# Layer 2 attention with probabilities left unnormalised: reciprocal sums spread, transposed and multiplied into the heads

## The chip, the cores and the metric

The kernel runs on one core of a Trainium2 chip. It is one program for four layers of a small transformer. The metric is the device time of one execution in microseconds (us). Its engines work in parallel, each through its own queue in order, and meet at semaphores: PE is TensorE (matrix products and transposes, from SBUF to the eight PSUM banks), DVE is VectorE, ACT is ScalarE, POOL is GpSimd, SP issues transfers.

## The reference

Activations are four batch rows of 512 tokens and 128 channels. Each layer has an attention and a feed-forward part, each behind a layer norm with modulation and a gate. The change touches only the attention of layer 2, with 16 heads of 64:

```python
q = apply_rope(split_heads(x @ Wq)); k = apply_rope(split_heads(x @ Wk)); v = split_heads(x @ Wv)
sim = jnp.einsum('bid,bjd->bij', q, k) * scale
sim = jnp.where(causal[None], sim, -jnp.inf)
attn = jax.nn.softmax(sim, axis=-1)
out = jnp.einsum('bij,bjd->bid', attn, v)
out = out.reshape(b, h, t, d).transpose(0, 2, 1, 3).reshape(b, t, h * d)
return out @ Wo + bo
```

## The kernel before

The stage works in 32 units, one for each batch row (`B` = 4) and pair of heads (`PAIRS` = 8). In a unit, 128 partitions hold two heads of 64 channels, and the 512 tokens are four tiles of 128 (`TB` = 4). The software pipeline is written out by hand: in round u of every engine's loop (from -2 to 32) unit u+2 is projected, unit u+1 gets its scores and exponentials, unit u is transposed and multiplied with the values, and unit u-1 is projected out and added to the residual `x`. The source's order is the order of each queue; the only other order is by the semaphores.

The steps, by their functions:

- `att_project` (L991, L994): q, k (one 512-wide product each) and v (four 128-wide ones) into bank 0. `att_rope` on DVE (L1124, L1125) multiplies and swaps out of bank 0, and POOL (L1201, L1206) multiplies and adds to `q_rope` and `k_rope`.
- `att_scores` (L1007): causal scores of both heads, in three steps of 512 keys (query tile 3), 384 and 128 (tiles 2 and 0) and 256 (tile 1), into banks 1 to 4. `att_maxes` on DVE (L1134) masks and takes row maxima. `att_exps` on ACT (L1079) writes exponentials to `soft` and row sums to `exp_sum`.
- `norm`: on DVE (L1152 reciprocal, L1145 product) for the first head and half of the second; on POOL (L1215) for tiles 3 and 2 of the second. It scales `soft` in place.
- `att_transpose` (L1021): the 20 blocks of 128x128 below the diagonal, in five groups f = 0 to 4 (`FILLS`) of four blocks. Group n of the whole run goes into bank 5 + n % 2; ACT copies it to `softT` (L1091).
- `att_values` (L1033): values of both heads into bank 7, channels by tokens. DVE copies them to `head_out` (L1164, `heads`).
- `att_output` (L1039): output projection of the pair, bank 7 again; DVE adds it to `x` with the gate (L1174, `add`; L1170 adds the bias once per batch row).

So the order of PE in round u is: scores step 0 of u+1, q projection of u+2, output of u-1, transposes f = 0 of u, scores step 1, f = 1, k projection, f = 2, scores step 2, f = 3, v projection, f = 4, values.

Of the kernel before, what the change touches and what calls it, by code (L numbers as in the profile page):

```python
# [20 lines left out]
B = 4  # L21
# [41 lines left out]
def adaln_blocks(nc, d, out):  # L63

    ctx = ExitStack()
    with ctx:
# [899 lines left out]
        exp_sum = tmp_sb("exp_sum", [128, 2, 8])  # L966
        exp_inv = tmp_sb("exp_inv", [128, 2, 8])
        head_out = [tmp_sb(f"head_out{i}", [128, T]) for i in range(2)]
# [43 lines left out]
        def att_transpose(pe, u, f):  # L1012
            if f < 2:
                pe.wait_ge(sem("p_normed"), 2 * u + f + 1)
            if f == 1:
                pe.wait_ge(sem("p_normed_pool"), u + 1)
            if 5 * u + f >= 2:
                pe.wait_ge(sem("pt_ready"), 5 * u + f - 1)
            for i, (hd, jc, t) in enumerate(FILLS[f]):
                at = TILE_AT[t] + 128 * jc  # L1020
                last = pe.transpose(bank[5 + (5 * u + f) % 2][:, 128 * i:128 * i + 128],  # L1021
                                    soft[u % 2][:, hd, at:at + 128], ident[:, :])
            last.then_inc(sem("pt_raw"), 1)

        def att_values(pe, u):
            if u:
                pe.wait_ge(sem("pair_added"), added(u - 1))
            pe.wait_ge(sem("proj_read"), 3 * u + 3)
            for jc, fills in ((0, 2), (1, 4), (3, 4), (2, 5)):
                pe.wait_ge(sem("pt_ready"), 5 * u + fills)  # L1030
# [53 lines left out]
        def att_act(act):  # L1084
            nc.scalar.preload_act_table_set("natural_log_exp_and_others")

            def transposed(u, f):
                if f == 0 and u:
                    act.wait_ge(sem("pv_raw"), B + u)
                act.wait_ge(sem("pt_raw"), 5 * u + f + 1)  # L1090
                nc.scalar.activation(softT[:, 512 * f:512 * f + 512], bank[5 + (5 * u + f) % 2][:, :], ACT.Copy) \  # L1091
                  .then_inc(sem("pt_ready"), 1)

            def values(u):
                act.wait_ge(sem("proj_raw"), 3 * u + 3)
                if u >= 3:
                    act.wait_ge(sem("pv_raw"), B + u - 2)
                nc.scalar.activation(v_tok[u % 3][:, :, :], bank[0][:, :].rearrange("p (i c) -> p i c", i=TB),
                                     ACT.Copy).then_inc(sem("proj_read"), 1)

            for u in range(-2, UNITS + 1):
                score, project, work = 0 <= u + 1 < UNITS, u + 2 < UNITS, 0 <= u < UNITS
                if score:
                    att_exps(act, u + 1, 0)
                if work:
                    transposed(u, 0)
                    transposed(u, 1)
                if score:
                    att_exps(act, u + 1, 1)
                if work:  # L1110
                    transposed(u, 2)
                    transposed(u, 3)
                if score:
# [23 lines left out]
        def att_dve(dve):  # L1137
            def norm(u):
                par = u % 2

                def tiles(hd, ts):
                    for t in ts:
                        n = stat_at(t, hd)
                        p = soft[par][:, hd, TILE_AT[t]:TILE_AT[t] + keys(t)]
                        last = nc.vector.tensor_scalar(p, p, exp_inv[:, par, n:n + 1], None, ALU.mult)  # L1145
                    return last

                if u >= 2:
                    dve.wait_ge(sem("p_normed_pool"), u - 1)
                for half in range(2):  # L1150
                    dve.wait_ge(sem("s_exp"), 8 * u + STEP_END[1 + half])
                    nc.vector.reciprocal(exp_inv[:, par, 4 * half:4 * half + 4], exp_sum[:, par, 4 * half:4 * half + 4]) \  # L1152
                      .then_inc(sem("s_inv"), 1)
                    dve.wait_ge(sem("s_inv"), 2 * u + half + 1)
                    if half == 0:
                        tiles(0, (3, 2))
                tiles(0, (0, 1)).then_inc(sem("p_normed"), 1)
                tiles(1, (0, 1)).then_inc(sem("p_normed"), 1)
# [20 lines left out]
            for u in range(-2, UNITS + 1):  # L1179
                score, project, out = 0 <= u + 1 < UNITS, u + 2 < UNITS, u >= 1  # L1180
                if out:
                    heads(u - 1)
                if score:
# [3 lines left out]
                if out:  # L1187
                    add(u - 1)
                if score:
                    att_maxes(dve, u + 1, 1)  # L1190
                if project:
                    att_rope(dve, u + 2, 1)
                if score:
                    att_maxes(dve, u + 1, 2)
                    norm(u + 1)

        def att_pool(pool):
# [11 lines left out]
            pool.wait_ge(sem("att_tables"), 32)  # L1209
            def norm(u):  # L1210
                pool.wait_ge(sem("s_inv"), 2 * u + 1)
                for t in (3, 2):
                    n = stat_at(t, 1)
                    p = soft[u % 2][:, 1, TILE_AT[t]:TILE_AT[t] + keys(t)]
                    last = nc.gpsimd.tensor_tensor(p, p, exp_inv[:, u % 2, n:n + 1].to_broadcast([128, keys(t)]), ALU.mult)  # L1215
                last.then_inc(sem("p_normed_pool"), 1)

            for u in range(UNITS):
                rope(u, 0)
                rope(u, 1)  # L1220
                if u >= 1:
                    norm(u - 1)
            norm(UNITS - 1)

# [1041 lines left out]
```

## Time and profile before

| | us |
|---|---|
| median of 3 runs | 1713.69 (1708.1 to 1717.39) |
| the profiled execution | 1712.15 |
| its span in the profile | 1710.3 |

| engine | busy us | share of the span | instructions |
|---|---|---|---|
| PE | 1280.4 | 75% | 10366 |
| DVE | 1093.0 | 64% | 2509 |
| ACT | 829.1 | 48% | 2019 |
| POOL | 623.6 | 36% | 577 |

The layer 2 attention is the stretch from about 382 to 782 us of the span. The shares above are averages over stages with different limits, so this stage has to be read by itself. In a timeline a row is a run of like instructions: its start, the time from the first start to the last end, how many, and in brackets what ended an idle time. An fp32 product shows as two instructions on PE, and a next one starts before the one ahead of it has ended, so the distance between starts tells how long a group holds the engine.

### The profile page before, as it was taken

How to read it: one execution, taken by the hardware profiler on the slowest of the kernel's cores; microseconds unless marked ns; L12 is line 12 of the kernel's file. 1: busy time of each engine (PE TensorE's matmuls, PEld its weight loads, DVE VectorE, ACT ScalarE, POOL GpSimd, SP SyncE). 2: the span in 40 equal slices, each digit the busy share in tenths (PEclk: the TensorE clock that was granted, in tenths of full speed). 3: DMA queues.
4: the chain of work that ended last, by engine and by line, in shares of the span. 5: the costliest groups of instructions: out<-in, count | busy, mean ns of one | idle time of the engine just before them, and what ended most of it. 6: DMA issues, size and time to landing. Idle time of an engine off the chain costs nothing.

```text
span 1710.3 us, 27876 instructions
## 1 busy us (share of the span) xinstructions
PE 1280.4 (75%) x10366; PEld 734.0 (43%) x10366; DVE 1093.0 (64%) x2509; ACT 829.1 (48%) x2019; POOL 623.6 (36%) x577
## 2 busy tenths in 40 slices
PE   8754009548999999996878888767777687777768
PEld 6222009514555555552345555434444433444433
DVE  4366503227999999994257777646776644677653
ACT  4651003124566665664666666545555434555542
POOL 1110160345565565652012222145555404555520
PEclk8966559757999999998999999869999997999989
DMA  7000115560000000002000000000000000000000
GB/s 252 1 0 0 48 40 202 125 69 1 1 1 1 1 1 1 1 1 87 0 1 2 2 2 2 1 27 1 2 2 2 2 1 1 2 2 2 1 2 25
DMA packets 15265, 38.95 MB, mean 23 GB/s; under 512 B 3572, under 2 KB 8054, under 8 KB 14496
## 3 DMA queue, kind: packets, MB, share of 16 engines
q1 hardware_dynamic: 13088, 34.70, 5.7%
q0 software_dynamic: 2048, 2.54, 2.1%
q8 instruction: 80, 1.31, 0.3%
q14 instruction: 49, 0.40, 0.1%
HBM read 33.07 MB, written 5.77 MB: 23 GB/s over the span
## 4 chain that ended last, share of the span: by engine, by line
PE 37%; DVE 31%; ACT 15%; issue 10%; POOL 4%; DMA 1%; SPq 0%; DVEq 0%; POOLq 0%; ACTq 0%
DVE soft L1145 6%; DVE bank L1134 5%; PE bank L1694 4%; PE bank L1377 4%; ACT win_soft_alibi L1384 3%; PE bank L1359 3%; ACT win_soft_local L1384 3%; PE bank L1916 3%; DVE rope_part L1125 3%; PE bank L1349 2%; PE bank L195 2%; ACT win_softT_alibi L1392 2%; PE bank L1702 2%; PE bank L1713 2%; PE bank L203 2%
## 5 line engine op out<-in xcount | busy, mean ns | idle before, releaser
L1079 ACT ACTIVATE soft<-bank,neg_max 128x512 f32<-128x512 f32 (+3 forms) x256 | 133.2, 535 | 123.9 <-DVE neg_max L1134 122.7
L1863 POOL TENSOR_TENSOR win_part<-win_part,scaled_tab 128x512 f32<-128x512 f32 x64 | 81.2, 1269 | 200.7 <-DVE win_part L1805 200.7
L1145 DVE TENSOR_SCALAR soft<-soft,exp_inv 128x128 f32<-128x128 f32 (+1 forms) x192 | 137.5, 768 | 2.2
L1694 PE MATMUL bank<-shifted,att_w 128*128 128x512 f32 x128 | 78.9, 748 | 78.2 <-DVE v_even L1832 69.1
L1201 POOL TENSOR_TENSOR rope_part<-rope_part,rope_tab 128x512 f32<-128x512 f32 x64 | 82.2, 1285 | 145.9 <-DVE rope_part L1125 145.8
L1419 POOL TENSOR_TENSOR win_soft_alibi<-win_soft_alibi,win_inv_alibi 128x384 f32<-128x384 f32 x64 | 52.9, 827 | 218.3 <-DVE win_inv_alibi L1403 218.3
L1134 DVE CUSTOM_DVE_ANT_0 bank<-bank,att_mask 128x512 f32<-128x512 f32 (+3 forms) x256 | 118.5, 512 | 6.9 <-PE bank L1007 6.9
L1091 ACT ACTIVATE softT<-bank 128x512 f32<-128x512 f32 x160 | 93.6, 612 | 26.5 <-PE bank L1021 26.5
L1021 PE MATMUL bank<-ident,soft 128*128 128x128 f32 x640 | 99.7, 279 | 1.9 <-ACT softT L1091 1.9
L1007 PE MATMUL bank<-k_rope,q_rope 64*128 64x128 f32 (+3 forms) x512 | 97.6, 479 | 2.2 <-POOL k_rope L1206 2.2
L1384 ACT ACTIVATE win_soft_local<-bank,win_neg_max_local,rq 128x128 f32<-128x128 f32 x256 | 96.2, 463 | 5.7 <-DVE win_neg_max_local L1815 5.7
L1419 POOL TENSOR_TENSOR win_soft_local<-win_soft_local,win_inv_local 128x512 f32<-128x512 f32 x64 | 78.7, 1231 | 55.1 <-DVE win_inv_local L1403 55.1
L1021 PEld LDWEIGHTS bank<-ident,soft 128*128 128x128 f32 x640 | 74.0, 141 | 50.0 <-issue 42.7
L1751 ACT ACTIVATE win_sq_local<-bank 128x512 f32<-128x512 f32 x64 | 38.2, 597 | 112.0 <-PE bank L1694 112.0
L251 DVE TENSOR_TENSOR ln_norm<-bank,ln_rstd 128x512 f32<-128x512 f32 x40 | 27.7, 692 | 100.2 <-ACT ln_rstd L239 94.9
L1392 ACT ACTIVATE win_softT_local<-bank 128x512 f32<-128x512 f32 x64 | 38.3, 598 | 107.1 <-PE bank L1359 107.1
L1392 ACT ACTIVATE win_softT_alibi<-bank 96x512 f32<-96x512 f32 x64 | 38.3, 598 | 87.6 <-PE bank L1359 87.6
L264 POOL TENSOR_SCALAR h<-ln_norm,mod 128x512 f32<-128x512 f32 x28 | 22.0, 785 | 152.6 <-DVE ln_norm L251 152.6
L1033 PE MATMUL bank<-softT,v_tok 128*64 128x128 f32 (+3 forms) x512 | 76.0, 439 | 0.0
L991 PE MATMUL bank<-h,att_w 128*128 128x512 f32 x128 | 72.4, 649 | 4.1 <-DVE ln_norm L251 2.2
L1804 DVE TENSOR_TENSOR win_part<-bank,scaled_tab 128x512 f32<-128x512 f32 x64 | 44.0, 687 | 49.0 <-ACT win_sq_local L1751 49.0
L1691 PE MATMUL bank<-att_w,shifted 128*128 128x128 f32 x256 | 40.0, 303 | 43.2 <-ACT log_q L1758 43.2
(329 smaller groups left out, 3331.0 us busy)
## 6 DMA issues: line engine op xcount, KB each, us to landing
moe_w<-in_moe_w SPq DMA_DIRECT2D x8, 960.0 KB, 6.1
y_tok<-in_moe_w SPq DMA_DIRECT2D x8, 960.0 KB, 5.6
att_w<-in_att_w SPq DMA_DIRECT2D x1, 1536.0 KB, 8.3
att_w<-in_local_w SPq DMA_DIRECT2D x1, 1536.0 KB, 8.9
xg_dram<-zeros SPq DMA_DIRECT2D x5, 256.0 KB, 9.2
y_dram<-y_slot SPq DMA_DIRECT2D x16, 80.0 KB
wmod<-in_wmod SPq DMA_DIRECT2D x1, 1152.0 KB, 7.6
x<-in_x SPq DMA_DIRECT2D x4, 256.0 KB, 4.6
```

The costliest lines, as they stand in the source:

```text
L1007: last = pe.matmul(score_bank(u, s, hd)[:, at:at + keys(t)], q_rope[u % 2][lo:lo + 64, 128 * t:128 * t + 128], k_rope[u % 2][lo:lo + 64, 0 ...
L1021: last = pe.transpose(bank[5 + (5 * u + f) % 2][:, 128 * i:128 * i + 128], soft[u % 2][:, hd, at:at + 128], ident[:, :])
L1079: nc.scalar.activation(soft[par][:, hd, TILE_AT[t]:TILE_AT[t] + keys(t)], score_bank(u, s, hd)[:, at:at + keys(t)], ACT.Exp, scale=-1.0, b ...
L1091: nc.scalar.activation(softT[:, 512 * f:512 * f + 512], bank[5 + (5 * u + f) % 2][:, :], ACT.Copy) \
L1134: nc.vector.tensor_tensor_reduce(sc, sc, att_mask[:, T - keys(t):T], -1.0, 3e38, ALU.add, ALU.min, neg_max[:, u % 2, n:n + 1]).then_inc(se ...
L1145: last = nc.vector.tensor_scalar(p, p, exp_inv[:, par, n:n + 1], None, ALU.mult)
L1201: nc.gpsimd.tensor_tensor(rope_part[2 * piece + 1][:, :], rope_part[2 * piece + 1][:, :], rope_tab[:, 2 * piece + 1, :], ALU.mult).then_in ...
L1384: nc.scalar.activation(a["soft"][u % 2][:, j, :], bank[2 + half][:, 128 * k:128 * k + a["keys"]], ACT.Exp, bias=a["neg_max"][:, u % 2, j:j ...
L1392: nc.scalar.activation(a["softT"][0:a["keys"], 512 * half:512 * half + 512], bank[4 + 3 * half][0:a["keys"], :], ACT.Copy).then_inc(sem("w ...
L1419: nc.gpsimd.tensor_tensor(a["soft"][u % 2][:, js, :], a["soft"][u % 2][:, js, :], a["inv"][:, u % 2, js].unsqueeze(2).to_broadcast([128, 4 ...
L1694: last = pe.matmul(bank[5 * piece][:, :], w, tokens(b, 0, T), start=True, stop=True)
L1863: nc.gpsimd.tensor_tensor(swapped, swapped, scaled_tab[:, 2 * j + 1, :], ALU.mult) \
```

## The change

The exponentials stay unnormalised. DVE takes one reciprocal of the eight row sums of a unit (`invert`). POOL spreads them to `inv_wide`, 64 copies of each, so that four tiles of 128 partitions (queries) by 128 (two heads by 64) stand there (`spread`). PE transposes these four tiles into bank 6 (`att_sums`), ACT copies bank 6 to `sum_inv`, channels by tokens (`inverse`), and DVE multiplies the heads by it where it copied them before (`heads`). Bank 5 now takes f = 0, 2 and 4, bank 6 takes f = 1, 3 and the sums. The copy of f = 3 moves from ACT to DVE (`transposed` there). The output projection moves from ahead of f = 0 to behind f = 1. On DVE, `heads` moves behind the q rope and `add` behind the maxima of step 1.

```diff
         def att_transpose(pe, u, f):
-            if f < 2:
-                pe.wait_ge(sem("p_normed"), 2 * u + f + 1)
-            if f == 1:
-                pe.wait_ge(sem("p_normed_pool"), u + 1)
-            if 5 * u + f >= 2:
-                pe.wait_ge(sem("pt_ready"), 5 * u + f - 1)
+            if f == 0:
+                pe.wait_ge(sem("s_exp"), 8 * u + 8)
+            if f == 1 and u:
+                pe.wait_ge(sem("sum_inv"), u)
+            elif u or f > 1:
+                pe.wait_ge(sem("pt_ready"), 4 * u + max(f - 1, 0))
...
+        def att_sums(pe, u):
+            pe.wait_ge(sem("inv_spread"), u + 1)
+            for t in range(TB):
+                last = pe.transpose(bank[6][:, 128 * t:128 * t + 128], inv_wide[:, stat_at(t, 0):stat_at(t, 0) + 2, :].rearrange("p i c -> p (i c)"), ident[:, :])
+            last.then_inc(sem("sum_raw"), 1)
...
+                if jc == 1:
+                    pe.wait_ge(sem("pt_ready_dve"), u + 1)
...
-                if out:
-                    att_output(pe, u - 1)
                 if work:
                     att_transpose(pe, u, 0)
                 if score:
                     att_scores(pe, u + 1, 1)
                 if work:
                     att_transpose(pe, u, 1)
+                if out:
+                    att_output(pe, u - 1)
...
                     att_values(pe, u)
+                    att_sums(pe, u)
...
+            def inverse(u):
+                act.wait_ge(sem("sum_raw"), u + 1)
+                if u:
+                    act.wait_ge(sem("pv_read"), u)
+                nc.scalar.activation(sum_inv[:, :], bank[6][:, :], ACT.Copy).then_inc(sem("sum_inv"), 1)
...
                 if work:
                     transposed(u, 0)
+                if out:
+                    inverse(u - 1)
+                if work:
                     transposed(u, 1)
...
+            def invert(u):
+                dve.wait_ge(sem("s_exp"), 8 * u + 8)
+                if u:
+                    dve.wait_ge(sem("inv_spread"), u)
+                nc.vector.reciprocal(exp_inv[:, :], exp_sum[:, u % 2, :]).then_inc(sem("s_inv"), 1)
...
             def heads(u):
                 dve.wait_ge(sem("pv_raw"), B + u + 1)
                 if u >= 2:
                     dve.wait_ge(sem("att_out"), u - 1)
-                nc.vector.tensor_copy(head_out[u % 2][:, :], bank[7][:, :]).then_inc(sem("pv_read"), 1)
+                dve.wait_ge(sem("sum_inv"), u + 1)
+                nc.vector.tensor_tensor(head_out[u % 2][:, :], bank[7][:, :], sum_inv[:, :], ALU.mult) \
+                  .then_inc(sem("pv_read"), 1)
...
-                if out:
-                    heads(u - 1)
+                if 0 <= u < UNITS:
+                    invert(u)
                 if score:
                     att_maxes(dve, u + 1, 0)
                 if project:
                     att_rope(dve, u + 2, 0)
                 if out:
-                    add(u - 1)
+                    heads(u - 1)
                 if score:
                     att_maxes(dve, u + 1, 1)
+                if out:
+                    add(u - 1)
                 if project:
                     att_rope(dve, u + 2, 1)
+                if 0 <= u < UNITS:
+                    transposed(u, 3)
                 if score:
                     att_maxes(dve, u + 1, 2)
-                    norm(u + 1)
...
+            def spread(u):
+                pool.wait_ge(sem("s_inv"), u + 1)
+                if u:
+                    pool.wait_ge(sem("sum_raw"), u)
+                nc.gpsimd.tensor_copy(inv_wide[:, :, :], exp_inv[:, :].unsqueeze(2).to_broadcast([128, 8, 64])) \
+                  .then_inc(sem("inv_spread"), 1)
```

Left out above: the normalising on DVE and POOL, which goes; the buffers; the counts of `pt_ready`, now four a unit; and DVE's copy of f = 3, which reads bank 6 and counts `pt_ready_dve`.

On PE, at the start of a round in the middle of the stage, before; L1007 are scores, L991 a q or k projection, L1039 the output projection, L1021 the transposes:

```order
L1007 MATMUL bank<-k_rope,q_rope 128x512 [waits s_exp,roped]
L1007 MATMUL bank<-k_rope,q_rope 128x512
L991 MATMUL bank<-h,att_w 128x512 [waits proj_read]
L1039 MATMUL bank<-head_out,att_wo 128x512 [waits pv_read]
L1021 MATMUL bank<-ident,soft 128x128 [waits pt_ready,p_normed]
L1021 MATMUL bank<-ident,soft 128x128 x3
L1007 MATMUL bank<-k_rope,q_rope 128x384 [waits s_exp]
L1007 MATMUL bank<-k_rope,q_rope 128x384
L1007 MATMUL bank<-k_rope,q_rope 128x128 x2
L1021 MATMUL bank<-ident,soft 128x128 [waits pt_ready,p_normed_pool,p_normed]
```

And after, from the last three of the four transposes of the sums, L1029, at the end of the round ahead; L1009 are the scores, L993 the projections, L1023 the transposes and L1048 the output projection:

```order
L1029 MATMUL bank<-ident,inv_wide 128x128 x3
L1009 MATMUL bank<-k_rope,q_rope 128x512 [waits s_exp,roped]
L1009 MATMUL bank<-k_rope,q_rope 128x512
L993 MATMUL bank<-h,att_w 128x512 [waits proj_read]
L1023 MATMUL bank<-ident,soft 128x128 [waits pt_ready,s_exp]
L1023 MATMUL bank<-ident,soft 128x128 x3
L1009 MATMUL bank<-k_rope,q_rope 128x384 [waits s_exp]
L1009 MATMUL bank<-k_rope,q_rope 128x384
L1009 MATMUL bank<-k_rope,q_rope 128x128 x2
L1023 MATMUL bank<-ident,soft 128x128 [waits sum_inv]
L1023 MATMUL bank<-ident,soft 128x128 x3
L1048 MATMUL bank<-head_out,att_wo 128x512 [waits pv_read]
```

Four transposes stand new at the end of the round, f = 1 waits for the copied sums (`sum_inv`) where it waited for normalised probabilities, and the output projection stands behind it.

On ACT, from the wide exponentials (L1079) of a round, before; L1091 copies transposes:

```order
L1079 ACTIVATE soft,exp_sum<-bank,neg_max 128x512 [waits s_max] x2
L1091 ACTIVATE softT<-bank 128x512 [waits pt_raw,pv_raw]
L1091 ACTIVATE softT<-bank 128x512 [waits pt_raw]
L1079 ACTIVATE soft,exp_sum<-bank,neg_max 128x384 [waits s_max]
L1079 ACTIVATE soft,exp_sum<-bank,neg_max 128x128
```

And after; L1089 are exponentials, L1101 copies transposes and L1115 copies the sums:

```order
L1089 ACTIVATE soft,exp_sum<-bank,neg_max 128x512 [waits s_max] x2
L1101 ACTIVATE softT<-bank 128x512 [waits pt_raw,pv_raw]
L1115 ACTIVATE sum_inv<-bank 128x512 [waits pv_read,sum_raw]
L1101 ACTIVATE softT<-bank 128x512 [waits pt_raw]
L1089 ACTIVATE soft,exp_sum<-bank,neg_max 128x384 [waits s_max]
L1089 ACTIVATE soft,exp_sum<-bank,neg_max 128x128
```

The copy of the sums stands behind the two wide exponentials and the copy of f = 0, and ahead of the copy of f = 1.

## Rows read from the trace of the kernel before

**Rows 1.** Stretches: length, busy PE, PEld, DVE, ACT, POOL (instructions), PEclk, DMA, GB/s.

```profile
900.00:1080.00 180.00, 152.96 (x1945) 90.28 (x1944) 139.49 (x274) 114.32 (x323) 41.36 (x50) 1.00 0.01 2
500.00:594.00 94.00, 92.20 (x524) 50.26 (x522) 93.37 (x256) 58.64 (x176) 55.44 (x49) 1.00 0.00 1
```

**Rows 2.** Chain of waits, 509 to 533, shares by line.

```profile
by line: DVE soft L1145 28.4%; DVE bank L1134 23.4%; issue 12.0%; DVE rope_part L1125 11.9%; DVE rope_part L1124 8.1%; DVE head_out L1164 5.7%; DVE neg_max L1134 4.6%; DVE x L1174 3.3%; DVE x L1170 1.6%; DVE exp_inv L1152 1.2%; DVEq L1173 0
```

**Rows 3.** Timeline of PE, one unit: start, length, instruction, [idle before].

```profile
524.43 1.13 PE L1007 MATMUL bank<-k_rope,q_rope 64*128 64x512 f32 x4
...
526.49 1.12 PE L1039 MATMUL bank<-head_out,att_wo 128*128 128x512 f32 x2
527.45 0.60 PE L1021 MATMUL bank<-ident,soft 128*128 128x128 f32 x4
527.98 1.14 PE L1007 MATMUL bank<-k_rope,q_rope 64*128 64x384 f32 x8
529.04 0.66 PE L1021 MATMUL bank<-ident,soft 128*128 128x128 f32 x4
529.54 1.02 PE L991 MATMUL bank<-h,att_w 128*128 128x512 f32 x2
530.40 0.60 PE L1021 MATMUL bank<-ident,soft 128*128 128x128 f32 x4
...
531.56 0.66 PE L1021 MATMUL bank<-ident,soft 128*128 128x128 f32 x4
532.37 1.16 PE L994 MATMUL bank<-att_w,h 128*128 128x128 f32 x8
...
533.89 2.37 PE L1033 MATMUL bank<-softT,v_tok 128*64 128x512 f32 x16
536.20 0.70 PE L1007 MATMUL bank<-k_rope,q_rope 64*128 64x512 f32 x2
```

**Rows 4.** Timeline of DVE, the same unit.

```profile
526.35 0.68 DVE L1134 CUSTOM_DVE_ANT_0 bank<-bank,att_mask 128x512 f32<-128x512 f32 x1
526.96 0.14 DVE L1134 DVE_READ_ACCUMULATOR2_ANT neg_max<- 128x1 f32 x1
...
528.84 0.73 DVE L1174 SCALAR_TENSOR_TENSOR x<-bank,mod,x 128x512 f32<-128x512 f32 x1
...
532.22 0.42 DVE L1134 CUSTOM_DVE_ANT_0 bank<-bank,att_mask 128x256 f32<-128x256 f32 x1
...
532.94 0.17 DVE L1152 RECIPROCAL exp_inv<-exp_sum 128x4 f32<-128x4 f32 x1
...
537.51 0.68 DVE L1164 COPY head_out<-bank 128x512 f32<-128x512 f32 x1
```

**Rows 5.** Timeline of ACT, the same unit.

```profile
527.13 0.69 ACT L1079 ACTIVATE soft<-bank,neg_max 128x512 f32<-128x512 f32 x1 [3.71 <-DVE neg_max L1134]
...
528.47 0.59 ACT L1091 ACTIVATE softT<-bank 128x512 f32<-128x512 f32 x1
...
532.20 1.10 ACT L1091 ACTIVATE softT<-bank 128x512 f32<-128x512 f32 x2
```

**Rows 6.** Timeline of PE, the last two units.

```profile
763.98 0.60 PE L1021 MATMUL bank<-ident,soft 128*128 128x128 f32 x4
...
774.02 1.04 PE L1021 MATMUL bank<-ident,soft 128*128 128x128 f32 x8
```

**Rows 7.** Timeline of DVE, the last addition of the stage.

```profile
781.63 0.75 DVE L1174 SCALAR_TENSOR_TENSOR x<-bank,mod,x 128x512 f32<-128x512 f32 x1 [1.22 <-PE bank L1039]
```

**Rows 8.** Timeline of POOL, the unit of rows 3.

```profile
532.39 1.28 POOL L1201 TENSOR_TENSOR rope_part<-rope_part,rope_tab 128x512 f32<-128x512 f32 x1 [0.68 <-DVE rope_part L1125]
...
535.04 1.94 POOL L1215 TENSOR_TENSOR soft<-soft,exp_inv 128x512 f32<-128x512 f32 x2
```

**Rows 9.** Groups of POOL by form: count, busy us, mean ns, idle before.

```profile
L1215 POOL TENSOR_TENSOR soft<-soft,exp_inv 128x512 f32<-128x512 f32 x32 | 36.9, 1153 | 7.3 <-DVE exp_inv L1152 7.3
...
L264 POOL TENSOR_SCALAR h<-ln_norm,mod 128x512 f32<-128x512 f32 x28 | 22.0, 785 | 152.6 <-DVE ln_norm L251 152.6
```

More of the change, by code:

```diff
@@ L966, in adaln_blocks @@
         exp_sum = tmp_sb("exp_sum", [128, 2, 8])
-        exp_inv = tmp_sb("exp_inv", [128, 2, 8])
+        exp_inv = tmp_sb("exp_inv", [128, 8])
+        inv_wide = tmp_sb("inv_wide", [128, 8, 64])
+        sum_inv = tmp_sb("sum_inv", [128, T])
         head_out = [tmp_sb(f"head_out{i}", [128, T]) for i in range(2)]
@@ L1012, in att_transpose @@
         def att_transpose(pe, u, f):
-            if f < 2:
-                pe.wait_ge(sem("p_normed"), 2 * u + f + 1)
-            if f == 1:
-                pe.wait_ge(sem("p_normed_pool"), u + 1)
-            if 5 * u + f >= 2:
-                pe.wait_ge(sem("pt_ready"), 5 * u + f - 1)
+            if f == 0:
[4 more added lines that the diff above has]
+                pe.wait_ge(sem("pt_ready"), 4 * u + max(f - 1, 0))
             for i, (hd, jc, t) in enumerate(FILLS[f]):
                 at = TILE_AT[t] + 128 * jc
-                last = pe.transpose(bank[5 + (5 * u + f) % 2][:, 128 * i:128 * i + 128],
-                                    soft[u % 2][:, hd, at:at + 128], ident[:, :])
+                last = pe.transpose(bank[5 + f % 2][:, 128 * i:128 * i + 128], soft[u % 2][:, hd, at:at + 128], ident[:, :])
             last.then_inc(sem("pt_raw"), 1)
+        def att_sums(pe, u):
[3 more added lines that the diff above has]
+            last.then_inc(sem("sum_raw"), 1)
         def att_values(pe, u):
@@ L1028, in att_values @@
             pe.wait_ge(sem("proj_read"), 3 * u + 3)
-            for jc, fills in ((0, 2), (1, 4), (3, 4), (2, 5)):
-                pe.wait_ge(sem("pt_ready"), 5 * u + fills)
+            for jc, fills in ((0, 2), (1, 3), (3, 3), (2, 4)):
+                pe.wait_ge(sem("pt_ready"), 4 * u + fills)
+                if jc == 1:
+                    pe.wait_ge(sem("pt_ready_dve"), u + 1)
                 for hd in range(2):
@@ L1090, in transposed @@
                 act.wait_ge(sem("pt_raw"), 5 * u + f + 1)
-                nc.scalar.activation(softT[:, 512 * f:512 * f + 512], bank[5 + (5 * u + f) % 2][:, :], ACT.Copy) \
+                nc.scalar.activation(softT[:, 512 * f:512 * f + 512], bank[5 + f % 2][:, :], ACT.Copy) \
                   .then_inc(sem("pt_ready"), 1)
@@ L1099, in values @@
                                      ACT.Copy).then_inc(sem("proj_read"), 1)
+            def inverse(u):
[3 more added lines that the diff above has]
+                nc.scalar.activation(sum_inv[:, :], bank[6][:, :], ACT.Copy).then_inc(sem("sum_inv"), 1)
             for u in range(-2, UNITS + 1):
-                score, project, work = 0 <= u + 1 < UNITS, u + 2 < UNITS, 0 <= u < UNITS
+                score, project, work, out = 0 <= u + 1 < UNITS, u + 2 < UNITS, 0 <= u < UNITS, u >= 1
                 if score:
@@ L1111, in att_act @@
                     transposed(u, 2)
-                    transposed(u, 3)
                 if score:
@@ L1137, in att_dve, with transposed @@
         def att_dve(dve):
[L1138 to L1158, printed above, removed]
+            def invert(u):
[3 more added lines that the diff above has]
+                nc.vector.reciprocal(exp_inv[:, :], exp_sum[:, u % 2, :]).then_inc(sem("s_inv"), 1)
+            def transposed(u, f):
+                if u:
+                    dve.wait_ge(sem("pv_raw"), B + u)
+                dve.wait_ge(sem("pt_raw"), 5 * u + f + 1)
+                nc.vector.tensor_copy(softT[:, 512 * f:512 * f + 512], bank[5 + f % 2][:, :]).then_inc(sem("pt_ready_dve"), 1)
             def heads(u):
@@ L1209, in att_pool @@
             pool.wait_ge(sem("att_tables"), 32)
[L1210 to L1216, printed above, removed]
+            def spread(u):
+                pool.wait_ge(sem("s_inv"), u + 1)
+                if u:
+                    pool.wait_ge(sem("sum_raw"), u)
+                nc.gpsimd.tensor_copy(inv_wide[:, :, :], exp_inv[:, :].unsqueeze(2).to_broadcast([128, 8, 64])) \
+                  .then_inc(sem("inv_spread"), 1)
             for u in range(UNITS):
@@ L1220, in att_pool @@
                 rope(u, 1)
-                if u >= 1:
-                    norm(u - 1)
-            norm(UNITS - 1)
+                if u >= 2:
+                    spread(u - 2)
+            spread(UNITS - 2)
+            spread(UNITS - 1)
         next_block()
```

## The prediction

> **What bounds the kernel now.** I read the busy time by stretch first, then the chain of waits, then each engine's timeline through one steady unit (a pair of heads of one batch row) of the layer 2 attention. In 94 us, eight such units, DVE is busy 93.37 us, PE 92.20, ACT 58.64 and POOL 55.44, and TensorE is granted its full clock, 1.00 [rows 1]. The chain of waits runs along DVE, and its largest share, 28.4%, is the normalisation, L1145 [rows 2]. So DVE sets the beat. PE stands right behind it, though, which has to be read from starts, since matmuls overlap and their lengths add up to more than their time. The unit runs from the scores at 524.43 to the next unit's at 536.20: 11.77 us. Every group of PE begins where the one before hands over, except the value projection at 532.37: the four transposes before it began at 531.56, and such a group holds PE for 0.53 (527.45 to 527.98), to 532.09. So PE idles 0.28 us a unit, and its own work, hand-overs included, is 11.77 - 0.28 = 11.49 us [rows 3]. What the reader is to see: taking work from DVE can win 0.28 us a unit at most, and work added to PE eats that at once.
>
> **What the change takes from DVE.** From the first reciprocal at 532.94 to the head copy at 537.51 lie 4.57 us of normalising [rows 4]. All of it goes. In its place stand one reciprocal (0.17 as at 532.94, 0.20 with its hand-over) and one copy of transposes, 0.61 like the distance of the wide PSUM operation at 526.35 to the next at 526.96. The multiplication of the heads takes the place of the head copy: 0.68, from PSUM, as that copy and as the wide operation. DVE falls to 11.77 - 4.57 + 0.20 + 0.61 = 8.0 us a unit and no longer bounds. POOL changes two products for one spread; ACT one copy of transposes for the copy of the sums, so its load is the same.
>
> **What it adds to PE.** Four 128x128 transposes, `att_sums`: 0.53. PE's own work becomes 11.49 + 0.53 = 12.02 us. Even with no new wait the unit is 0.25 longer than now.
>
> The Trainium skill, "TensorE: Matmul & The Clock Gate", Part 4 (PE-mode transpose), gives about 275 ns for a 128x128 transpose in one kernel's context. By that figure the four would be an estimated 1.10 us, and the whole 17 us slower than my sum, about 1768. The trace disagrees with it as a price: four take 0.60 from first start to last end and hold the next group for 0.53 [rows 3].
>
> **The waits it adds.** The transposed sums lie in bank 6. The second group of transposes of the next unit, f = 1, needs that bank, so PE waits there for `sum_inv`, which ACT writes; and ACT issues that copy only after the two wide exponentials of the next unit and the copy of f = 0. Counted from the start of the wide scores (0):
> - scores end at 1.13 [rows 3]; DVE's first row maximum is handed out 0.61 + 0.14 = 0.75 after its start [rows 4]; a hand-over is 0.03 from DVE to ACT (526.96 + 0.14 = 527.10, to 527.13) [rows 4, 5], and I take 0.04 to 0.05, an estimate from that, for those that end at PE and DVE. ACT begins at 1.13 + 0.04 + 0.75 + 0.03 = 1.95.
> - two wide exponentials: 527.13 to 528.47 = 1.34, to 3.29. Then two PSUM copies back to back, f = 0 and the sums: 1.10 (532.20) [rows 5], to 4.39. PE may go on at about 4.43.
> - PE is there after scores and projection (2.06, less 0.04, since a wide product before transposes holds 0.96), transposes and scores (527.45 to 529.04 = 1.59): 3.61. It waits **0.82**.
> - Behind f = 1 now stands the output projection. It needs the heads, which DVE multiplies once `sum_inv` is there: 4.39 + 0.05 + 0.68 + 0.05 = 5.17, while f = 1 ends its hold at 4.43 + 0.53 = 4.96. PE waits **0.21** more.
> Queued behind both is everything else of the unit, in order, on PE: nothing hides them. Then: output 0.86 (the hold of a wide product after transposes, 529.54 to 530.40), to 6.03; k projection 0.96, to 6.99; the rest of the unit from 530.40 to 536.20 without its gap, 5.52, to 12.51; the sums 0.53: **13.04 us a unit, 1.27 more than 11.77**.
>
> **Do the other engines keep up at 13.04?** DVE after the heads (from 4.43, slot 0.61): the old stretch 528.84 to 532.22, add, maxima and k rope, 3.38 [rows 4], ends at 8.42. Its PSUM reads are over at about 8.5; the value projection wants them at 8.68 (6.99, and 530.40 to 532.09 = 1.69). POOL: product and sum of k, 532.39 to 535.04 = 2.65 [rows 8], from 8.58 to 11.23. The sums are wanted at 12.51, so the spread may take 1.23. No row shows it: a one-input 512-wide operation is 0.79, the wide product with the same kind of spread operand is 1.15 [rows 9], and it writes 512 elements like both. Below 0.79 nothing is gained and up to 1.15 nothing is lost; what is beyond is a rival. I take 0.8 and no wait. The copy of f = 3 on DVE shifts the last exponentials, yet their chain ends about 0.4 before the last values ask.
>
> **The sum.** There are 32 units, 31 intervals and a tail. Units 1 to 28: 28 x 1.27 = 35.6. The first interval has neither output nor inverse: 12.02 - 0.86 = 11.16, -0.6. Interval 29 has no q projection: 12.08, +0.3. The last, from 763.98 to 774.02 = 10.04 before [rows 6], has no projections either, but the same chain for `sum_inv`: f = 1 at 3.4, output 0.74 behind it, then 0.96 + 1.69, some 0.6 of waiting for copies, and transposes, values (533.89 to 536.20 = 2.31 [rows 3]) and sums, 0.53 + 2.31 + 0.53: 10.7, +0.7. The tail was 774.02 to 781.63 = 7.61 [rows 6, 7]. Now f = 1 waits for the sums (1.8), the previous output and its heads come before the rest (3.4), three groups with their copies carry to 5.2, the values to 7.5, and sums, copy, heads and output follow one by one (0.6, 0.65, 0.7, 1.2): 10.7, +3.1. Together +39 us. The profiled execution took 1712.15 us (span 1710.3), 1.5 less than the median of the runs shown, 1713.69. 1712.15 + 39.1 = **1751**.
>
> **Rivals.**
> - *Only the added work, no wait* (10%). The order of ACT speaks against it; for it, that ACT idles 3.71 before the wide exponentials now [rows 5], so it might be early. Then 28 x 0.25 = 7, ends as above but half the tail: about 1720.
> - *The spread is slow* (12%): POOL ends late and PE waits for it before the sums. At 1.6 us the unit grows by 0.37: 29 x 0.37 = 11, 1762. From 1.23 on each tenth costs 3 us.
> - *The clock falls* (7%), since PE now stops about 1 us in each unit. Against it: in the stretch from 900 to 1080 PE is busy 152.96 of 180 us, 85%, at 1.00 [rows 1], and here it would be 92%. At 1.2 GHz a stretch gives half the work; a tenth of the 420 us would cost 21: 1772.
> - *Faster* (3%): PE's 11.49 is not work but following DVE closely, and gives way once DVE is early. It decides at the hand-overs: if PE's hold per unit could fall below DVE's. Then DVE's 8.0 with the two waits, 9.0, sets the unit: 28 x 2.7 = 76 less, about 1637. Against it, groups that wait for nothing DVE does start in the same lock step.
>
> The Trainium skill, "Trainium Kernel Development and Optimization", Performance Expectations, calls the busy share of weight loads a good metric and that of matmuls a bad one. Loads are busy 50.26 of the 94 us, 53% [rows 1]; by that rule PE has room, the last rival. The starts in the timeline say otherwise.
>
> **How the numbers follow.** Forecast 68%: 1751, its own range 1742 to 1760 (0.3 us a unit, most of it in the two waits and the hand-overs). With the slow spread and part of the clock case above it: 1738 to 1768. What a measurement of this kernel can tell from no change is about 0.5%, 1705 to 1722. Slower: forecast, spread, clock and the upper part of the first rival, 89%. Same: the rest of it, 7%. Faster 4%.
>
> **What would show it.** In the profile after: units 13.0 apart; DVE busy some 61% of the stage and PE some 92%; PE idle about 0.8 before f = 1 behind ACT's copy of the sums, and 0.2 before the output projection behind DVE's heads; no wait at the sums; clock 1.00. Wrong would be: a wait at the sums behind POOL, no wait at f = 1, PE groups that hold for another time than now, or a lower clock.

## The result and the profile after

| | us |
|---|---|
| kernel before, median of 4 runs | 1715.54 (1708.10 to 1717.95) |
| changed kernel, median of 4 runs | 1749.80 (1745.48 to 1753.14) |
| ratio | 1.0206, 95% interval 1.0165 to 1.0246 |
| profiled execution, span | 1747.1 (before 1710.3) |

The change made the kernel slower by 2.1% (1.65% to 2.46%); the forecast was 1751.

First the busy time of a stretch of about eight units, read as [rows 1]:

```profile
500.00:604.40 104.40, 96.64 (x559) 54.51 (x557) 66.80 (x209) 59.54 (x176) 45.17 (x40) 1.00 0.00 1
```

DVE went from 99% of the stretch to 64%; PE stands at 93%, at the full clock. Both stretches hold the first unit of a batch row, which is longer than the steady ones: 12.35 us before and 13.67 after, where the steady ones are 11.77 and 13.11. The chain of waits over two units, as [rows 2], has changed its engine:

```profile
by line: PE bank L1042 17.7%; PE bank L1009 13.2%; PE bank L1023 11.2%; issue 9.7%; PE bank L1048 8.7%; PE bank L996 7.2%; ACT soft L1089 7.0%; PE bank L993 6.6%; DVE head_out L1173 5.4%; PE bank L1029 4.1%; ACT sum_inv L1115 3.8%; ACT soft
```

Where L1145 and L1134 of DVE led, PE's lines lead. One unit on PE answers to [rows 3]. It begins with the four transposes of the sums at 537.46, then the scores at 538.04:

```profile
537.46 0.66 PE L1029 MATMUL bank<-ident,inv_wide 128*128 128x128 f32 x4
538.04 1.13 PE L1009 MATMUL bank<-k_rope,q_rope 64*128 64x512 f32 x4
539.11 1.12 PE L993 MATMUL bank<-h,att_w 128*128 128x512 f32 x2
540.07 0.60 PE L1023 MATMUL bank<-ident,soft 128*128 128x128 f32 x4
540.60 1.14 PE L1009 MATMUL bank<-k_rope,q_rope 64*128 64x384 f32 x8
542.49 0.66 PE L1023 MATMUL bank<-ident,soft 128*128 128x128 f32 x4 [0.76 <-ACT sum_inv L1115]
543.32 1.12 PE L1048 MATMUL bank<-head_out,att_wo 128*128 128x512 f32 x2 [0.17 <-DVE head_out L1173]
544.28 1.02 PE L993 MATMUL bank<-h,att_w 128*128 128x512 f32 x2
...
550.57 0.66 PE L1029 MATMUL bank<-ident,inv_wide 128*128 128x128 f32 x4
551.15 1.13 PE L1009 MATMUL bank<-k_rope,q_rope 64*128 64x512 f32 x4
```

From scores to scores it is 13.11 us. Two starts carry a note. f = 1 at 542.49 waited for `sum_inv`: the scores ahead of it, at 540.60, hold 1.06 us [rows 3], so it could have begun at 541.66 and lost 0.83. The output projection at 543.32 waited for the heads: f = 1 holds 0.49, so it lost 0.34. (The notes give 0.76 and 0.17, since they count from the modelled end of the group ahead, which lies behind its hold.) There is no other note in a steady unit.

ACT, as [rows 5], shows who made `sum_inv` late. It idles 3.44 us, then works through two wide exponentials and the copy of f = 0, and only then copies the sums, 541.83 to 542.43:

```profile
540.01 0.69 ACT L1089 ACTIVATE soft<-bank,neg_max 128x512 f32<-128x512 f32 x1 [3.44 <-DVE neg_max L1152]
...
541.36 0.59 ACT L1101 ACTIVATE softT<-bank 128x512 f32<-128x512 f32 x1
541.83 0.60 ACT L1115 ACTIVATE sum_inv<-bank 128x512 f32<-128x512 f32 x1
```

DVE, as [rows 4], is idle before the maxima and before the heads, and nobody waits for its 2.08 us in front of the reciprocal:

```profile
537.01 0.20 DVE L1160 RECIPROCAL exp_inv<-exp_sum 128x8 f32<-128x8 f32 x1 [2.08 <-POOL inv_wide L1227]
539.22 0.70 DVE L1152 CUSTOM_DVE_ANT_0 bank<-bank,att_mask 128x512 f32<-128x512 f32 x1 [2.01 <-PE bank L1009]
...
542.57 0.69 DVE L1173 TENSOR_TENSOR head_out<-bank,sum_inv 128x512 f32<-128x512 f32 x1 [0.75 <-ACT sum_inv L1115]
```

POOL, as [rows 8], has the spread done at 536.91, 0.55 before PE begins the transposes of the sums at 537.46. The operation that no row of before showed takes 0.62 us, less than either neighbour in [rows 9]:

```profile
533.65 1.28 POOL L1214 TENSOR_TENSOR rope_part<-rope_part,rope_tab 128x512 f32<-128x512 f32 x1 [2.74 <-DVE rope_part L1143]
535.07 1.27 POOL L1219 TENSOR_TENSOR k_rope<-rope_part 128x512 f32<-128x512 f32 x1
536.29 0.62 POOL L1227 COPY inv_wide<-exp_inv 128x512 f32<-128x512 f32 x1
```

The last addition of the stage, which [rows 7] has at 781.63:

```profile
824.49 0.75 DVE L1184 SCALAR_TENSOR_TENSOR x<-bank,mod,x 128x512 f32<-128x512 f32 x1 [1.22 <-PE bank L1048]
```

It begins 42.9 us later. From f = 0 of the first unit (407.79 before, 409.90 after) to that addition the stage took 373.84 and takes 414.59 us, 40.7 more. The 2.1 ahead of it, which are there already at the first projection (383.49 and 385.61), and the rest of the program (from that start to the end of the span 928.7 before, 922.6 after) were not touched. Over the runs of this study that rest lay between 920 and 931 us without relation to the edits. So the 6 us by which the rest got shorter are such scatter, and the stage alone accounts for all of the loss.

### The profile page after: what moved, and what is told of

The parts are those of the page before. It is cut to its first block, busy times and chain, and to the rows that moved or that the text cites. A ratio compares the mean times of both kernels' runs of the same rounds, so it can differ in the third digit from the quotient of the medians.

```text
span 1747.1 us, 27972 instructions
## 1 busy us (share of the span) xinstructions
PE 1315.1 (75%) x10462; PEld 770.5 (44%) x10494; DVE 994.1 (57%) x2317; ACT 834.6 (48%) x2019; POOL 580.1 (33%) x545
## 4 chain that ended last, share of the span: by engine, by line
PE 51%; ACT 18%; DVE 15%; issue 10%; POOL 4%; DMA 2%; SPq 0%; DVEq 0%; ACTq 0%; POOLq 0%
PE bank L1042 4%; PE bank L1390 4%; PE bank L1707 4%; PE bank L1009 3%; ACT win_soft_alibi L1397 3%; PE bank L1372 3%; ACT win_soft_local L1397 3%; PE bank L1929 3%; PE bank L1023 2%; PE bank L195 2%; PE bank L1362 2%; ACT win_softT_alibi L1405 2%; PE bank L1715 2%; PE bank L1726 2%; PE bank L203 2%
## 5 line engine op out<-in xcount | busy, mean ns | idle before, releaser
L1089 ACT ACTIVATE soft<-bank,neg_max 128x512 f32<-128x512 f32 (+3 forms) x256 | 132.3, 525 | 158.9 <-DVE neg_max L1152 158.9
L1023 PE MATMUL bank<-ident,soft 128*128 128x128 f32 x640 | 99.6, 278 | 25.6 <-ACT sum_inv L1115 24.9
L1707 PE MATMUL bank<-shifted,att_w 128*128 128x512 f32 x128 | 72.9, 698 | 53.5 <-DVE v_even L1845 44.3
L1023 PEld LDWEIGHTS bank<-ident,soft 128*128 128x128 f32 x640 | 73.7, 141 | 76.2 <-issue 43.6
L1009 PE MATMUL bank<-k_rope,q_rope 64*128 64x128 f32 (+3 forms) x512 | 96.9, 476 | 2.1 <-POOL k_rope L1219 2.1
L1101 ACT ACTIVATE softT<-bank 128x512 f32<-128x512 f32 x128 | 76.6, 599 | 27.8 <-PE bank L1023 27.8
L1704 PE MATMUL bank<-att_w,shifted 128*128 128x128 f32 x256 | 53.9, 377 | 44.3 <-ACT log_q L1771 44.3
L993 PE MATMUL bank<-h,att_w 128*128 128x512 f32 x128 | 72.3, 648 | 4.1 <-DVE ln_norm L251 2.2
L222 ACT ACTIVATE ln_square<-bank 128x512 f32<-128x512 f32 x40 | 23.8, 594 | 99.6 <-PE bank L195 99.2
```

Of the source, the lines that this page charges most:

```text
L1009: last = pe.matmul(score_bank(u, s, hd)[:, at:at + keys(t)], q_rope[u % 2][lo:lo + 64, 128 * t:128 * t + 128], k_rope[u % 2][lo:lo + 64, 0 ...
L1023: last = pe.transpose(bank[5 + f % 2][:, 128 * i:128 * i + 128], soft[u % 2][:, hd, at:at + 128], ident[:, :])
L1089: nc.scalar.activation(soft[par][:, hd, TILE_AT[t]:TILE_AT[t] + keys(t)], score_bank(u, s, hd)[:, at:at + keys(t)], ACT.Exp, scale=-1.0, b ...
L1707: last = pe.matmul(bank[5 * piece][:, :], w, tokens(b, 0, T), start=True, stop=True)
```

## The experiments

All but one were timed together with the kernel before, whose median there was between 1707.12 and 1710.39. So ratios are compared, and the unit, from one unit's first wide scores to the next's in the middle of a batch row, which repeats within 0.02 us but for the two runs whose unit is set by transfers.

### The copy of the sums ahead of the exponentials

```diff
+                if out:
+                    inverse(u - 1)
                 if score:
                     att_exps(act, u + 1, 0)
                 if work:
                     transposed(u, 0)
-                if out:
-                    inverse(u - 1)
```

> The changed kernel with one edit: ACT copies the transposed sums at the start of its round, ahead of the two wide exponentials, where it idles 3.44 us. Theory (the two waits make the loss beyond PE's own work): f = 1 waits no more (0.83 us a unit now); the output projection waits some 0.25 for the heads, which stand behind the q rope on DVE; the unit falls from 13.11 to 12.24, the time to about 1723. Rival (the wait only shows where PE is late anyway): the idle time moves to another group, the unit stays at 13.1, the time at 1750.

Measured: 1723.61 us, ratio 1.0090 (1.0073 to 1.0107), unit 12.25. PE, from the scores over f = 1 (547.57) and the output projection (548.35) to the next scores:

```profile
543.95 1.13 PE L1009 MATMUL bank<-k_rope,q_rope 64*128 64x512 f32 x4
...
547.57 0.66 PE L1023 MATMUL bank<-ident,soft 128*128 128x128 f32 x4
548.35 1.13 PE L1048 MATMUL bank<-head_out,att_wo 128*128 128x512 f32 x2
549.31 1.02 PE L993 MATMUL bank<-h,att_w 128*128 128x512 f32 x2
...
556.19 1.13 PE L1009 MATMUL bank<-k_rope,q_rope 64*128 64x512 f32 x4
```

The wait of f = 1 is gone. The output projection follows f = 1 by 0.78 where 0.49 is the hold: 0.29 are left for the heads. The wait was paid in full: 0.86 us came back in each steady unit from one moved copy. The first unit of a batch row gained only 0.27 (13.67 to 13.40); the run that turns eight columns comes back to it.

### Heads first on DVE as well

```diff
                 if 0 <= u < UNITS:
                     invert(u)
+                if out:
+                    heads(u - 1)
                 if score:
                     att_maxes(dve, u + 1, 0)
                 if project:
                     att_rope(dve, u + 2, 0)
-                if out:
-                    heads(u - 1)
```

> As the run before, and DVE also multiplies the heads ahead of the row maxima and the q rope. Theory: no wait is left, PE's own work with the four transposes sets the unit, 12.0 to 12.05; time 1714 to 1720, no faster than the kernel before. Rival (PE only follows DVE, whose load is 8 us): the unit falls well under 11.77, to 9 or 10, the time under 1670.

Measured: 1711.94 us, ratio 1.0026 (1.0015 to 1.0036), unit 11.90:

```profile
537.83 1.13 PE L1009 MATMUL bank<-k_rope,q_rope 64*128 64x512 f32 x4
...
549.15 0.66 PE L1029 MATMUL bank<-ident,inv_wide 128*128 128x128 f32 x4
549.73 1.13 PE L1009 MATMUL bank<-k_rope,q_rope 64*128 64x512 f32 x4
```

The second wait is gone too, and the unit comes to rest 0.13 above the 11.77 of before, though 0.1 below the 12.0 that I expected. The rival by which PE only follows DVE falls: DVE is busy 66.50 of 95.20 us here, some 8.3 a unit.

### Without the path of the sums

```diff
                     att_values(pe, u)
-                    att_sums(pe, u)
...
-                nc.vector.tensor_tensor(head_out[u % 2][:, :], bank[7][:, :], sum_inv[:, :], ALU.mult) \
+                nc.vector.tensor_copy(head_out[u % 2][:, :], bank[7][:, :]) \
```

(and no `invert`, `spread`, `inverse`; f = 1 waits for DVE's copy of f = 3 instead; heads first.)

> The changed kernel without the path of the sums: no reciprocal, spread, transposes of the sums, copy of them; the heads are copied as before and stand first on DVE. It leaves out the division by the row sums. Theory: the unit is PE's old work, 11.45 to 11.5, though DVE is at 8 us; the time 1702 to 1706, so relieving DVE fully is worth 0.3 us a unit. Rival (PE follows DVE): a unit of 9 to 10, under 1670.

Measured: 1692.16 us, ratio 0.9930 (0.9905 to 0.9954), unit 11.27, below the 11.45 to 11.5 of the theory, as is the time. PE, with the groups whose hold differs from [rows 3]:

```profile
533.06 1.12 PE L993 MATMUL bank<-h,att_w 128*128 128x512 f32 x2
...
535.62 0.66 PE L1023 MATMUL bank<-ident,soft 128*128 128x128 f32 x4
536.11 1.02 PE L1048 MATMUL bank<-head_out,att_wo 128*128 128x512 f32 x2
536.97 1.02 PE L993 MATMUL bank<-h,att_w 128*128 128x512 f32 x2
537.83 0.60 PE L1023 MATMUL bank<-ident,soft 128*128 128x128 f32 x4
...
539.00 0.66 PE L1023 MATMUL bank<-ident,soft 128*128 128x128 f32 x4
539.49 1.11 PE L996 MATMUL bank<-att_w,h 128*128 128x128 f32 x8
540.43 0.60 PE L1023 MATMUL bank<-ident,soft 128*128 128x128 f32 x4
...
544.33 1.12 PE L993 MATMUL bank<-h,att_w 128*128 128x512 f32 x2
```

From the q projection at 533.06 to the next at 544.33 is the unit. The output projection holds 0.86 (536.11 to 536.97), the v projection 0.94 (539.49 to 540.43) and f = 3 0.49 (539.00 to 539.49), where before has 0.96, 0.99 and where I took 0.53; the q projection holds 0.96, where before has 1.00 (525.49 to 526.49). So of the 0.22 us too many that I had counted as PE's work, 0.04 was a hold taken too long (the gap behind f = 3 was 0.32), and the rest was waiting that showed no idle time. The weight loads (PEld) of the output projection, before and here, show it:

```profile
526.48 0.30 PEld L1039 LDWEIGHTS bank<-head_out,att_wo 128*128 128x128 f32 x2 [0.69 <-DVE head_out L1164]
...
536.00 0.30 PEld L1048 LDWEIGHTS bank<-head_out,att_wo 128*128 128x128 f32 x2
```

Before, the load starts with its product (526.49), behind DVE's heads; here it starts 0.11 ahead of it (536.11), under the group in front. A group whose first weights are loaded only when it starts holds longer; one whose weights are loaded ahead holds shorter.

### The kernel before with four more transposes

```diff
             pe.wait_ge(sem("proj_read"), 3 * u + 3)
+            for i in range(TB):
+                pe.transpose(bank[7][:, 128 * i:128 * i + 128], soft[u % 2][:, 0, 128 * i:128 * i + 128], ident[:, :])
```

> The kernel before with four more 128x128 transposes a unit on PE, ahead of the values, into the bank that the values then overwrite; all else as before. Theory: PE's 11.49 + 0.53 = 12.02 passes DVE's 11.77; the unit is 12.0 to 12.05, the time 8 us more than before, about 1723. Rival (PE has room, as the 53% of its weight loads would have it): no change, 1715.

Measured: 1709.08 us, ratio 1.0005 (0.9991 to 1.0019), unit 11.77. The theory as I had it falls. The new transposes at 534.90 and 546.68, 11.78 apart:

```profile
534.47 0.60 PE L1021 MATMUL bank<-ident,soft 128*128 128x128 f32 x4
534.90 0.60 PE L1030 MATMUL bank<-ident,soft 128*128 128x128 f32 x4
535.43 2.37 PE L1035 MATMUL bank<-softT,v_tok 128*64 128x512 f32 x16
...
539.76 1.02 PE L1041 MATMUL bank<-head_out,att_wo 128*128 128x512 f32 x2
540.62 0.60 PE L1021 MATMUL bank<-ident,soft 128*128 128x128 f32 x4
...
546.68 0.60 PE L1030 MATMUL bank<-ident,soft 128*128 128x128 f32 x4
```

They begin 0.43 after those ahead and hold 0.53 (to 535.43), yet the unit did not grow: next to other transposes a group adds 0.43. PE's own work before was 11.27, with 0.43 more 11.70, and that fits under DVE's 11.77. The output projection now holds 0.86 (539.76 to 540.62) instead of 0.96, since the heads are there before PE is.

### The spread three times as long

```diff
+                for again in range(2):
+                    nc.gpsimd.tensor_copy(inv_more[again][:, :, :], exp_inv[:, :].unsqueeze(2).to_broadcast([128, 8, 64]))
                 nc.gpsimd.tensor_copy(inv_wide[:, :, :], exp_inv[:, :].unsqueeze(2).to_broadcast([128, 8, 64])) \
```

> The changed kernel with POOL writing the spread three times, the first two into other buffers: 1.86 us instead of 0.62. Theory (the sums wait for POOL once the spread passes the 1.17 from its start to the transposes of the sums): PE waits 0.7 there, the unit goes from 13.11 to 13.8, the time 20 us up. Rival (POOL's time is never on the path): the unit stays at 13.1.

Measured, one run: 1766.47 us, unit 13.71. The transposes of the sums wait for POOL now:

```profile
544.01 0.66 PE L1030 MATMUL bank<-ident,inv_wide 128*128 128x128 f32 x4 [0.52 <-POOL inv_wide L1230]
```

The two more spreads put off the last one by 1.10 us (542.24 to 543.34), and the unit grew by 0.60, where I expected 0.7. So POOL had some 0.5 us of room, and a spread longer than that would have been paid for in full: the rival with the slow spread was right in its mechanism, and only its condition did not hold.

### The sums by transfers

```diff
+        def att_sp(sp):
+            for u in range(UNITS):
+                sp.wait_ge(sem("s_inv"), u + 1)
+                sp.dma_start(inv_dram.rearrange("s p -> p s"), exp_inv[:, :], allow_slow_non_contiguous=True).then_inc(sem("inv_out"), 16)
...
+                for hd in range(2):
+                    sp.dma_start(sum_inv[64 * hd:64 * hd + 64, :],
+                                 inv_dram[4 * hd:4 * hd + 4, :].rearrange("s p -> (s p)").unsqueeze(0).to_broadcast([64, T])) \
```

> The run without sums, with the division back by another way: DVE's reciprocals go to DRAM by one transfer of 128x8 single elements and come back by two transfers spread over 64 partitions each, issued by SP; PE, ACT and POOL have no part in it. Theory: the transfers have a round, some 11 us, and are not seen; the unit stays at the 11.27 of the run without sums, the time 15 us below the kernel before. Rival (two transfers and their waits take over 11 us): the head multiplication waits for them, the unit is their chain, over 11.8, and nothing is gained.

Measured: 1793.14 us, ratio 1.0511 (1.0490 to 1.0531), units of 11.3 to 17.9, in the mean 14.1. The median time to landing of its transfers:

```profile
sum_inv<-inv_dram SPq DMA_DIRECT2D x64, 128.0 KB, 3.5
...
inv_dram<-exp_inv SPq DMA_DIRECT2D x32, 4.0 KB, 10.0
```

10.0 us for 4 KB in 1024 single elements, and 3.5 for the way back: 13.5 us and their waits for each other are the unit. The rival was right.

### The sums by transfers, with the output projection early

```diff
+                if out:
+                    att_output(pe, u - 1)
                 if work:
                     att_transpose(pe, u, 0)
...
                     att_rope(dve, u + 2, 0)
+                if out:
+                    add(u - 1)
                 if score:
                     att_maxes(dve, u + 1, 1)
-                if out:
-                    add(u - 1)
```

> As the run before, with the output projection ahead of f = 0 and the addition behind the q rope, as in the kernel before. Theory: the steady unit stays at 11.27, and the first unit of a batch row, 12.80 in the run without sums, falls to about 11.9, since the bias addition on DVE no longer stands right ahead of the k rope: 3 us less in all. Rival (the long first unit comes from elsewhere): 12.8 stays.

The edit puts `att_output` and `add` where the kernel before has them. Measured: 1785.55 us, ratio 1.0464 (1.0449 to 1.0478), units again set by the transfers, 13.9 in the mean. What it was to tell of the first units is hidden by that; the run that turns eight columns comes back to it.

### The copy of f = 3 back on ACT

```diff
                     transposed(u, 2)
+                    transposed(u, 3)
```

(on ACT, with DVE's call left out; otherwise the run with the heads first.)

> The run with the heads first (11.90 us a unit), with the copy of f = 3 back on ACT. Theory: both engines have room, the unit stays at 11.9, the move of this copy brought and cost nothing. Rival (the copy on ACT delays the last exponentials, or on DVE the maxima): the unit changes by 0.2 or more.

Measured: 1711.49 us, ratio 1.0037 (1.0025 to 1.0050), unit 11.91. In a kernel without the two waits, the move of that copy brought nothing and cost nothing.

### Eight columns turned instead of 512

```diff
+        def att_turn(pe, u):
+            pe.wait_ge(sem("s_inv"), u + 1)
+            pe.transpose(score_bank(u, 2, 0)[0:8, 256:384], exp_inv[:, :], ident[:, :]).then_inc(sem("inv_turned"), 1)
...
+                sp.dma_start(inv_dram, inv_row[:, :]).then_inc(sem("inv_out"), 16)
```

> As the run with the output projection early and the sums by transfers, but the transfer of single elements (10.0 us) goes: PE transposes the 128x8 reciprocals themselves into the idle half of a score bank at the end of the round, ACT copies the 8x128, and SP sends these to DRAM and back. Theory (the 13.6 us of the two transfers were the unit): the chain shrinks to some 7 us and fits the round; PE carries one transpose of 8 columns instead of four of 128, so the unit is 11.27 plus 0.1 to 0.2, some 11.4, and the time 9 us below the kernel before. Rival (the transfers stay too long or PE waits for the copy out of the score bank): over 11.77.

Measured: 1706.14 us, ratio 0.9965 (0.9945 to 0.9985), unit 11.52. The one transpose holds PE 0.20, as from 531.66 to 531.86:

```profile
531.66 0.27 PE L1044 MATMUL bank<-ident,exp_inv 128*8 128x128 f32 x1
531.86 1.13 PE L1012 MATMUL bank<-k_rope,q_rope 64*128 64x512 f32 x4
...
543.18 0.27 PE L1044 MATMUL bank<-ident,exp_inv 128*8 128x128 f32 x1
```

From 531.66 to 543.18 is the unit: 11.27, 0.20 for the transpose, and 0.05 for a v projection that holds longer again. I had expected 11.4, and 9 us less than before. Still, this keeps the idea of the change and is faster than the kernel before, by 0.35%.

The first unit of a batch row is 11.83 here, 0.3 above the others, where the run without sums had 12.80. The order of the output projection and the addition is not enough to explain it: the run with the heads first has the late order too, and 12.48. The bias addition on DVE, which only these units have, tells more. In the run without sums it takes 1.59 us, beside a product of POOL that starts with it:

```profile
513.16 1.59 DVE L1176 TENSOR_SCALAR x<-x,gate_bo 128x512 f32<-128x512 f32 x1
...
513.20 1.27 POOL L1213 TENSOR_TENSOR q_rope<-rope_part 128x512 f32<-128x512 f32 x1
```

In the first of the four such units of the same run it takes 0.48, and that unit is 11.70 instead of 12.80: the 1.1 us are the addition's. In the run that moved the copy of the sums it takes 1.08. In the other runs, but for one unit of the first run by transfers, it takes 0.46 to 0.49, and where a product of POOL starts within it, that one takes 1.41 to 1.57 instead of 1.27. So the order on DVE matters there by what POOL is doing at that moment.

### The kernel before with one product on ACT

```diff
-                        tiles(0, (3, 2))
+                        tiles(0, (3,))
...
+                if score:
+                    act.wait_ge(sem("s_inv"), 2 * (u + 1) + 1)
+                    n = stat_at(2, 0)
+                    p = soft[(u + 1) % 2][:, 0, TILE_AT[2]:TILE_AT[2] + keys(2)]
+                    nc.scalar.activation(p, p, ACT.Copy, scale=exp_inv[:, (u + 1) % 2, n:n + 1]).then_inc(sem("p_normed_act"), 1)
```

> The kernel before with one of its six DVE products of the normalisation, the 128x384 one of the first head, on ACT at the end of its round, where ACT idles; nothing else. Theory (before, DVE sets 11.77 and PE could do 11.27): DVE falls to about 10.6, PE sets the unit at 11.3 to 11.4, the time falls by 12 us. Rival (PE's own work is the 11.49 of the prediction): the unit is 11.5, the time 8 us less.

Measured: 1698.25 us, ratio 0.9942 (0.9920 to 0.9963), unit 11.44. It is the fastest version that computes everything, with PE busy 89.46 of 90 us and DVE below it:

```profile
500.00:590.00 90.00, 89.46 (x523) 50.58 (x522) 86.79 (x246) 61.90 (x184) 54.67 (x47) 1.00 0.01 1
```

Moving one of six products off DVE gave 0.33 us a unit. 11.44 lies between the theory (11.3 to 11.4) and the rival (11.5); the trace decides for the theory, since the 0.17 above 11.27 can be seen: f = 3 is followed after 0.61 instead of 0.49 by a v projection that waits for DVE, and that holds 0.99 instead of 0.94. DVE is busy 11.0 us a unit, not the 10.6 that I expected: its products of 128 and 256 columns, 0.56 and 0.63 us in the mean before, take 0.76 and 0.73 here.

## Why the prediction was right

- **DVE falls to 8.0 us a unit and no longer bounds**: it is busy 66.8 of 104.4 us, 8.4 a unit. Right but for 0.4; relieving it is worth 0.50 (11.77 to 11.27 without the sums), not the 0.28 that I gave as the most to win.
- **PE's own work, 11.49 + 0.53 = 12.02**: mis-sized. It was 11.27, and the sums cost 0.63 (11.90 in the run with the heads first): their hold of 0.58 (537.46 to 538.04) and 0.05 beside. Even with no wait the unit is longer than before, as I said, but by 0.13 and not 0.25. And PE had more room before than I saw: four more transposes, 0.43, were free there, though they would have used up nearly all of the 0.50.
- **f = 1 waits 0.82**: 0.83 in the trace, and 0.86 came back when ACT's copy was moved.
- **The output projection waits 0.21**: 0.34 in the trace, and 0.35 came back (12.25 to 11.90). It starts 0.83 behind f = 1 where I had 0.74: DVE issued the heads at 542.57, 0.14 after ACT's copy ended at 542.43, and I had given that hand-over 0.05. The projection itself then holds 0.96, not 0.86: its weights are loaded only when it starts (543.31), behind the heads.
- **The unit, 13.04**: 13.11. That it fits so well is in part luck: the terms that were too small and the one too large nearly cancelled, 11.90 + 0.86 + 0.35 against 12.02 + 0.82 + 0.21.
- **POOL keeps up**: right, with 0.62 for a spread that I had bounded by 0.79 and 1.15 and taken as 0.8. The true value lay below the nearest row, where it made no difference.
- **The sum, +39**: the stage grew by 40.7 us. By starts of f = 0: the first interval changed by -1.5 (12.58 before, 11.06 after; I had -0.6, counted from 11.77), the next 29 by +37.9 (343.61 and 381.53; I had 35.9), the last by +0.8 (10.04 and 10.86; I had 0.7), and the tail by +3.5 (7.61 and 11.14; I had 3.1). I did not count the first units of the batch rows apart; they grew by 1.32, about as much as the others. The untouched parts took 4.0 off the difference of the spans, which the forecast could not know.
- **The rivals**: only the added work, no wait, is what the run with the heads first makes of the kernel, 0.26% above before (I had 0.4%); it needs two edits that the change did not have. The clock stayed at 1.00 in spite of about 1.2 us of waiting a unit. The one on the faster side, and the rule of the Trainium skill beside it, "Trainium Kernel Development and Optimization", Performance Expectations, fall as a measure of room here: loads were busy 50.58 of 90 us, 56%, in the fastest full version, whose unit is 0.17 above PE's own work. There was some truth in the rival, 0.22 us.
- On the other rule of the Trainium skill, "TensorE: Matmul & The Clock Gate", Part 4: the transposes of the sums are 0.27 us long in the median, near its 275 ns, but four of them hold PE for 0.58, and four others for 0.43 to 0.53, not for 1.10.

## What to carry to other kernels

When two engines stand within a few per cent of each other, taking work from the first is worth only the distance to the second; to measure that distance, leave the work out or add some to the second, since starts in step can hide waiting. A result that crosses engines on its way costs nothing as long as it is there when it is asked for (the spread had 0.5 us of room), and what makes it late can be what stands ahead of it in an in-order queue: one copy issued behind two exponentials cost 0.86 us in each steady unit. Look for the smallest object to move: turning 8 columns instead of 512 left the idea a gain.

## What was not expected of the hardware

- On POOL a copy with a spread source writes 128x512 fp32 in 0.62 us, where the product with such an operand takes 1.15 [rows 9].
- On PE a group whose first weights are loaded only when it starts holds 0.05 to 0.1 us more without an idle time: a 512-wide product 0.96 instead of 0.86, eight 128-wide instructions 0.99 instead of 0.94. A wait for a semaphore is one cause; the q projection behind the scores loads its weights at its start too (539.10 after, with no wait noted) and holds 0.96, and no run shows why.
- A `tensor_scalar` operation of DVE on fp32 in SBUF and a product of POOL did not run side by side. The bias addition, 128x512 in 0.46 to 0.49 us, took 1.08 and 1.59 where it started beside a product of POOL, and ended 0.3 after it. A reciprocal of 128x4 showed no such wait (532.94, 0.17). In the kernel before, the normalising on DVE shows the same: its 128x512 and 128x384 products, 0.81 from 533.14 and 1.43 from 533.87, end 0.2 to 0.3 after POOL's products of 532.39 to 533.67 and 533.81 to 535.08. The narrower one takes longer, also in the mean:

```profile
L1145 DVE TENSOR_SCALAR soft<-soft,exp_inv 128x384 f32<-128x384 f32 x32 | 45.4, 1418 | 0.0
```

  So part of the 4.57 us of normalising in the prediction was waiting for POOL; how much, no run here separates.
- A transfer of 1024 single fp32 elements from 128 partitions took 10.0 us to land (median of 32). The same 4 KB in eight rows, with its way back, fitted a unit of 11.52 us.
